# Three of six product halves on GpSimd in fp32, the other three on VectorE with one operand in PSUM

## The chip, the cores and the metric

One core of a Trainium2 chip runs the whole network. The metric is the device time of one execution in microseconds (us), the median of three runs. The engines are TensorE (PE, with PEld for its weight loads), VectorE (DVE), ScalarE (ACT), GpSimd (POOL) and SyncE (SP, which here issues DMAs).

## The reference, cut to what matters

The network is a chain of layers on x of 16 x 128 x 128: a mixture of experts, an attention, a low-rank adapter, a **quantised feed-forward net**, four more layers. The change lies in the quantised net alone. Its reference:

```python
def act_qdq(x):
    qmax = 2.0 ** (ACT_BITS - 1) - 1.0
    scale = jnp.maximum(jnp.max(jnp.abs(x)) / qmax, 1e-12)
    return jnp.clip(jnp.round(x / scale), -qmax - 1.0, qmax) * scale
...
up = act_qdq(x @ lpbq_dequant(w_up).T)
gate = act_qdq(x @ lpbq_dequant(w_gate).T)
sig = fixed_qdq_u16(jax.nn.sigmoid(gate))
gate = act_qdq(gate * sig)
o = act_qdq(gate * up)
return o @ lpbq_dequant(w_down).T
```

Here up and gate are 384 x 2048 numbers each; the second gate is called gated below, and gated * up is called ot. `act_qdq` has 16 bits and one scale for the whole tensor. Every one needs the largest absolute value of its whole tensor before one number of it can be rounded, so the stage is a row of barriers: a maximum over all columns, then over the partitions (a transpose on TensorE), then a scale and its reciprocal, then rounding.

## The kernel before, in words

The order of each engine's work is written out by hand, one function per engine (`tensor`, `scalar`, `vector`, `gpsimd`, `sync`); engines meet through counting semaphores, and each engine runs its instructions strictly in the order written. The semaphores of one writer share a counter (`LANES`), so the counts there follow the counts of the instructions.

Data of the stage: `UP[0..2]` and `GT[0..2]` are 128 x 2048 fp32 tiles in SBUF, which hold up and gate * sigmoid; `G16` and `U16Q` are int16 tiles of the same shapes. `BK[0..7]` are the eight PSUM banks of 128 x 512 words. `RQ` holds the reciprocals of the scales, `rq(2)` for up and `rq(3)` for gated. `pieces` cuts the three tiles into four: the two halves of tile 0 (1024 columns each), tile 1 and tile 2 (2048 columns each).

The steps around the change, with their lines:

- ACT, L1008: three instructions of 2048 columns scale and round `UP` to int16 (`U16Q`), signal `up16`. They need only the scale of up (`quant` 6), which is there early.
- DVE, L1519: multiplies gate and sigmoid and takes the maximum (signal `gated_ff`, 5 pieces). Then L1459, the transpose on PE (L588, `quant_turn(3)`), L1463 to L1475 make the scale of gated (`quant` 9), and L1542 signals `ffs` 3.
- DVE, L1544: rounds the first piece of `GT` to int16 itself. ACT, L1012: rounds the other three pieces (1024, 2048 and 2048 columns), signal `gated16`.
- DVE, L1548 and L1456 (`absmax`, a helper; called in L1550): for each of the four pieces the product of two int16 operands into fp32 `GT`, and then its maximum, signals `ot_ff` and `o_max`.
- PE, L610 to L615: waits for `o_max` 3, issues eight matmuls whose result nobody reads (L612), then the transpose of the maximum (L588, `quant_turn(4)`, which waits for `part_max` 5), and then six more such matmuls (L615).
- DVE, L1459, L1463 to L1475, L1556: the scale of ot. ACT, L1016: 12 x rounding to int16 of 512 columns. DVE, L1561 and L1563: the two fp16 parts of each. PE, L625: the down projection, 36 matmuls into `BK[0..3]`. DVE, L1567: adds to x.
- GpSimd, L1865 and L1867: halves the eight pieces of the last layer's weights into two fp16 parts. Pieces 0 to 3 are done at `l_lo` 4, pieces 4 to 7 wait for `o_lo` 12 (the last L1563).
- SP, L1942: loads expert weights for a later layer; those of experts 8 to 11 go into the tile `RC`, where `U16Q` lies, and wait for `ot_ff` 4. Behind them in SP's queue are `halve(6)` and `halve(7)`, which wait for GpSimd's pieces 4 and 5.

Of the kernel before, what the change touches and what calls it, by code (L numbers as in the profile page):

```python
# [10 lines left out]
I32 = mybir.dt.int32  # L11
I16 = mybir.dt.int16
U16 = mybir.dt.uint16
ALU = mybir.AluOpType
ACT = mybir.ActivationFunctionType
X_AX = mybir.AxisListType.X

NB, S, D = 16, 128, 128
# [9 lines left out]
MAGIC = 12582912.0  # L28
# [26 lines left out]
    (("x4mm", 4), ("spread", 4), ("xtmm", 4)),  # L55
    (("quant_mm", 5), ("pttmm", 4)),

    (("gelu", 48), ("u0", 4), ("v", 8), ("lora", 4), ("ff", 24), ("up16", 3), ("o16", 12), ("x3", 4), ("su", 16), ("z_hi", 64)),
    (("ret_a", 1), ("fw_hi", 3), ("wbot", 8), ("l16", 4), ("sig_gates", 1), ("sigmoid", 4), ("sig_top", 2), ("gated16", 3), ("z", 4), ("x5", 4), ("qv_out", 8)),
    (("aw_hi", 1), ("xn_hi", 4), ("sig16", 5), ("vv", 4), ("sqr", 4), ("exp", 16)),  # L60
    (("route_exp", 2), ("theta", 1), ("q_sh", 4), ("sq", 4), ("rt_exp", 3), ("ptt", 4)),
    (("x_hi", 4), ("wt16", 1), ("wts0", 1), ("wts", 3), ("ot_hi", 3)),

    (("gated", 48), ("weff", 4), ("sin", 32), ("fw_lo", 3), ("k", 4), ("g", 8), ("x1", 4), ("l_max", 4), ("l_lo", 4),
     ("ff_max", 24), ("gate16", 4), ("gated_ff", 5), ("ot_ff", 4), ("o_lo", 12), ("x2", 4), ("pp", 4), ("w2", 2), ("weighed", 64), ("zw", 16)),
    (("xg", 4), ("kadd", 4), ("l_hi", 4), ("gated16_0", 1), ("o_max", 4), ("o_hi", 12), ("x4", 4), ("zlo", 64)),
    (("q", 4), ("sn", 1), ("part_max", 5), ("x3_lo", 4), ("rs", 4)),
    (("cent", 4), ("whole_max", 5), ("z_lo", 4), ("nm", 8)),
    (("const", 2), ("sh_lo", 2), ("sim_sq", 1), ("ffs", 4), ("k_out", 4)),
# [43 lines left out]
def program(nc, A, out):  # L113
    with ExitStack() as ctx:
        def sb(name, shape, dt=F32):
            return ctx.enter_context(nc.sbuf_tensor(name, shape, dt))
# [16 lines left out]
        BK = [ctx.enter_context(nc.psum_tensor(f"bk{i}", [128, 512], F32)) for i in range(8)]  # L133
# [52 lines left out]
        def cc(c):  # L186
            return slice(512 * c, 512 * c + 512)
# [79 lines left out]
        Q_AT, Q_STEPS = (0, 1, 2, 3, 0), (2, 4, 6, 9, 12)  # L267
# [20 lines left out]
        MX = QS  # L288
# [92 lines left out]
        def tensor(e):  # L381
            q = Eng(e, by_home)
# [145 lines left out]
            for t2 in range(8):  # L528
# [5 lines left out]
                for h in range(2):  # L534
# [3 lines left out]
                    t = e.matmul(o, ON3[:, :], BV3[:, 3, :], start=False, stop=True)  # L538
# [3 lines left out]
            for c in range(4):  # L542
                q.wait_ge("sin", 32)
                q.wait_ge(*(("v", 5 + c) if c < 2 else ("kadd", c - 1)))
                for i in range(4):
                    t = e.matmul(BK[c % 2][:, bb_(i)], qkv[:, 4 * c + i, :], qqv[:, 4 * c + i, :], start=True, stop=True)
# [32 lines left out]
            for c in range(4):  # L579
                q.wait_ge("x1", c + 1)  # L580
                q.wait_ge(*(("wbot", 7 + c) if c < 2 else ("k", 4)))
                for i in range(4):
                    t = e.matmul(BK[c][:, bb_(i)], WEFF[:, bb_(4 * c + i)], XT[:, bb_(4 * c + i)], start=True, stop=True)
# [23 lines left out]
                t.then_inc(S("ffmm"), 1)  # L607
            for i in range(1, 4):
                quant_turn(i)
            q.wait_ge("o_max", 3)  # L610
            for _ in range(8):
                e.matmul(BK[6][:, :], FW16[:, 0, 0, :], FW16[:, 0, 0:4, :], start=True, stop=True)  # L612
            quant_turn(4)
# [233 lines left out]
        def scalar(e):  # L847
# [145 lines left out]
            for i, (j, h) in enumerate(pieces):  # L993
# [9 lines left out]
                if i == 3:  # L1003
                    q.wait_ge("sig_top", 1)
                    e.activation(S16TOP, STOP, ACT.Copy, scale=65536.0).then_inc(S("sig_top"), 1)
            for j in range(3):
                q.wait_ge("quant", Q_STEPS[2])
                e.activation(U16Q[j], UP[j], ACT.Identity, scale=rq(2)).then_inc(S("up16"), 1)  # L1008
            for i, (j, h) in enumerate(pieces):
                if i:  # L1010
                    q.wait_ge("quant", Q_STEPS[3])
                    e.activation(G16[j][:, h], GT[j][:, h], ACT.Identity, scale=rq(3)).then_inc(S("gated16"), 1)  # L1012
            for j in range(3):
                for c in range(4):
# [114 lines left out]
        def vector(e):  # L1129
# [325 lines left out]
            def absmax(dst, src):  # L1455
                return red(dst, src, X_AX, ALU.max, apply_absolute_value=True)  # L1456

            def quant_part(i, parts):
                red(QS[:, 56 + Q_AT[i]:57 + Q_AT[i]], parts, X_AX, ALU.max).then_inc(S("part_max"), 1)  # L1459
# [80 lines left out]
            quant_whole(3)  # L1540
            quant_scale(3, U2)
            ts(U3, QS[:, 62:63], QS[:, 63:64], 1.0 / QMAX, ALU.mult, ALU.mult).then_inc(S("ffs"), 1)  # L1542
            j, h = pieces[0]
            ts(G16[j][:, h], GT[j][:, h], rq(3), None, ALU.mult).then_inc(S("gated16_0"), 1)  # L1544
            for i, (j, h) in enumerate(pieces):
                q.wait_ge(*(("gated16", i) if i else ("gated16_0", 1)))
                q.wait_ge("up16", j + 1)
                tt(GT[j][:, h], G16[j][:, h], U16Q[j][:, h], ALU.mult).then_inc(S("ot_ff"), 1)  # L1548
                q.wait_ge("ot_ff", i + 1)
                absmax(MX[:, 30 + i:31 + i], GT[j][:, h]).then_inc(S("o_max"), 1)  # L1550
            q.wait_ge("o_max", 4)
            q.wait_ge("ffs", 3)
            quant_part(4, MX[:, 30:34])
            quant_whole(4)
            quant_scale(4, U3)
            ts(SLW, QS[:, 60:61], 1.0 / WS, None, ALU.mult).then_inc(S("ffs"), 1)  # L1556
# [259 lines left out]

        def gpsimd(e):
            q = Eng(e, by_home)
            q.wait_ge("expert_lo", 16)
            q.wait_ge("c2b", 16)  # L1820
            for k in range(5):
                e.tensor_tensor(sl8(6 + k), sl8(1), C2B[:, k, :].unsqueeze(1).to_broadcast([128, 16, 8]), ALU.mult).then_inc(S("chosen"), 1)
            q.wait_ge("l1w", 16)
            q.wait_ge("l1m", 16)
            e.tensor_tensor(L1W, L1W, L1M, ALU.mult).then_inc(S("l1p"), 1)

            q.wait_ge("pk1", 16)
            q.wait_ge("col", 16)
            cosT, sinT = pk1("cos"), pk1("sin")
            for i, n in enumerate(("qq", "qk")):  # L1830
                o = 4 * i
                e.tensor_scalar(ROPE[:, o, :], cosT, col(n + "w"), None, ALU.mult).then_inc(S("rope"), 1)
                e.tensor_scalar(ROPE[:, o + 1, :], sinT, col(n + "ws"), None, ALU.mult).then_inc(S("rope"), 1)
                e.tensor_scalar(ROPE[:, o + 2, :], cosT, col(n + "b"), None, ALU.mult).then_inc(S("rope"), 1)
                e.tensor_scalar(ROPE[:, o + 3, :], sinT, col(n + "bs"), None, ALU.mult).then_inc(S("rope"), 1)
                q.wait_ge("rope", 5 * i + 4)
                e.tensor_tensor(ROPE[:, o + 2, :], ROPE[:, o + 2, :], ROPE[:, o + 3, :], ALU.add).then_inc(S("rope"), 1)
            q.wait_ge("pk0", 16)
            e.tensor_tensor(ATT[:, 0, :], pk0("relb"), pk1("amask"), ALU.add).then_inc(S("relm"), 1)

            q.wait_ge("rope", 10)
            q.wait_ge("down", UNITS)
            q.wait_ge("q", 4)
            for c in range(4):
                q.wait_ge("base", c + 1)
                for l in range(4 * c, 4 * c + 4):
                    for o, dst in ((0, QQ), (4, QK)):
                        e.tensor_scalar(dst[:, bb_(l)], BASE[:, bb_(l)], ROPE[:, o, l:l + 1], ROPE[:, o + 2, l:l + 1], ALU.mult, ALU.add).then_inc(S("cos"), 1)  # L1848

            for i, b in enumerate(HALVED):  # L1850
                q.wait_ge("k", 4)
                q.wait_ge("c2_hi", i + 1)
                e.tensor_tensor(GU16[b][:, 1, :], GU[b], GU16[b][:, 0, :], ALU.subtract).then_inc(S("c2_lo"), 1)


            q.wait_ge("sin", 32)
            q.wait_ge("fw_lo", 3)
            q.wait_ge("wbot", 8)
            q.wait_ge("route", BIASES)
            for i in range(8):  # L1860
                src = XF[:, 1024 * (i % 2):1024 * (i % 2) + 1024]
                q.wait_ge(*(("l_lo", 4) if i < 4 else ("o_lo", 12)))
                hi, lo = P16[:, 0, 1024 * i:1024 * i + 1024], P16[:, 1, 1024 * i:1024 * i + 1024]
                q.wait_ge(f"w2_{i % 2}", 16 * (i // 2 + 1))
                e.tensor_scalar(hi, src, 1.0, 1.0, ALU.mult, ALU.mult).then_inc(S("p16_hi"), 1)  # L1865
                q.wait_ge("p16_hi", i + 1)
                e.tensor_tensor(lo, src, hi, ALU.subtract).then_inc(S("p16"), 1)  # L1867

        def sync(e):
# [69 lines left out]
            for i in range(6):  # L1939
                halve(i)  # L1940
            for b in (0, 1, 2, 3, 8, 9, 10, 11):
                q.wait_ge(*(("ffs", 3) if b < 4 else ("ot_ff", 4)))  # L1942
                chosen(b)
            halve(6)
            halve(7)
# [129 lines left out]
```

## Time and profile before

| | |
|---|---|
| time, median of 3 runs (lowest to highest) | 490.58 us (490.44 to 490.92) |
| the profiled execution: its time | 490.49 us |
| its span, first to last instruction | 488.7 us |
| mean granted TensorE clock | 0.965 |
| busy: PE | 438.8 us, 90% |
| busy: DVE | 410.8 us, 84% |
| busy: ACT | 244.6 us, 50% |
| busy: POOL | 62.7 us, 13% |

The span is the time between the first and the last instruction of the profiled execution; 1.8 us of its time lie outside. Busy shares are means over the whole span and tell little of a stage that is 14 us long: there, the order of the instructions and their waits count. All times below are in us from the start of the span unless marked ns.

### The profile page before, as it was taken

What the parts mean: (1) busy time and instruction counts of PE and PEld (TensorE: products, weight loads), DVE (VectorE), ACT (ScalarE), POOL (GpSimd) and SP (SyncE); (2) the same over time, 40 slices, a digit from 0 to 9 for tenths busy, and PEclk for the clock granted to TensorE, in tenths of its full rate; (3) what the DMA queues carried; (4) which work ended last, traced back from release to release, by engine and by line L of the source; (5) the groups of instructions that cost most, each with busy time, mean ns of one, the idle gap of its engine ahead of it and who ended that gap; (6) DMA issues with size and microseconds to landing.
All of it is one profiled execution on the core that took longest, in us unless ns stands there. A gap on an engine that the chain in (4) does not pass through costs nothing.

```text
span 488.7 us, 9719 instructions
## 1 busy us (share of the span) xinstructions
PE 438.8 (90%) x3791; PEld 304.3 (62%) x3791; DVE 410.8 (84%) x919; ACT 244.6 (50%) x446; POOL 62.7 (13%) x77
## 2 busy tenths in 40 slices
PE   8999999998899989401899899999999999999997
PEld 6447999987358754100279876667656666655676
DVE  6997889777797659999876689986998999989786
ACT  5976555473856629895655554336224222423110
POOL 0007000000590705500081000000000000000000
PEclk9999999999999999855999998999999999999999
DMA  8979997950560003403330016545863000000000
GB/s 271 352 303 392 386 382 301 372 240 23 150 173 1 1 0 129 130 0 129 130 98 1 1 43 221 170 178 180 280 237 97 7 12 7 5 7 7 6 7 28
DMA packets 24629, 66.71 MB, mean 137 GB/s; under 512 B 3108, under 2 KB 6567, under 8 KB 24455
## 3 DMA queue, kind: packets, MB, share of 16 engines
q1 hardware_dynamic: 24144, 65.98, 37.7%
q8 instruction: 30, 0.49, 0.4%
q10 hardware_dynamic: 438, 0.11, 0.1%
q14 instruction: 17, 0.13, 0.1%
HBM read 38.68 MB, written 1.18 MB: 82 GB/s over the span
## 4 chain that ended last, share of the span: by engine, by line
PE 25%; DVE 25%; issue 4%; ACT 1%; DVEq 0%
PE bk L758 8%; DVE XT L1741 6%; DVE X L1729 4%; PE bk L766 4%; DVE RA L1769 4%; PE bk L803 3%; PE bk L625 2%; DVE RA L1548 1%; DVE WK L1590 1%; PE bk L778 1%; PE bk L634 1%; PE bk L668 1%; PE bk L685 1%; DVE QS L1456 1%; PE bk L694 1%
## 5 line engine op out<-in xcount | busy, mean ns | idle before, releaser
L758 PE MATMUL bk<-X,RB 128*128 128x512 f16 x384 | 94.6, 383 | 0.6 <-DVE X L1729 0.4
L1061 ACT ACTIVATE X<-RA 128x512 f16<-128x512 f32 x64 | 40.3, 630 | 100.9 <-DVE RA L1769 84.7
L1741 DVE SCALAR_TENSOR_TENSOR XT<-bk,WK,XT 128x128 f32<-128x128 f32 x192 | 67.0, 349 | 5.4 <-issue 0.2
L758 PEld LDWEIGHTS bk<-X,RB 128*128 128x128 f16 x384 | 37.0, 98 | 42.3 <-DVE X L1729 1.6
L766 PEld LDWEIGHTS bk<-RB,X 128*128 128x128 f16 x768 | 48.4, 98 | 15.4 <-issue 0.6
L766 PE MATMUL bk<-RB,X 128*128 128x128 f16 x768 | 53.5, 220 | 0.0
L1729 DVE TENSOR_TENSOR X<-RA,X 128x512 f16<-128x512 f32 x64 | 43.9, 685 | 1.1 <-ACT X L1061 1.1
L899 ACT ACTIVATE WK<-bk 128x512 f32<-128x512 f32 x48 | 28.6, 595 | 27.5 <-PE bk L414 21.9
L803 PE MATMUL bk<-RB,RA 128*128 128x512 f16 x144 | 38.8, 379 | 0.9 <-DVE RA L1786 0.9
L1357 DVE SCALAR_TENSOR_TENSOR RB<-WK,WCOL,bk 128x512 f32<-128x512 f32 x32 | 23.7, 744 | 10.0 <-ACT WK L899 10.0
L414 PE MATMUL bk<-X,RC 128*128 128x128 f16 x480 | 29.7, 219 | 0.0
L1363 DVE TENSOR_TENSOR RB<-RB 128x512 f16<-128x512 f32 x36 | 25.7, 715 | 3.9 <-ACT RB L909 3.6
L414 PEld LDWEIGHTS bk<-X,RC 128*128 128x128 f16 x480 | 27.9, 98 | 0.9
L909 ACT ACTIVATE RB<-RB 128x512 f16<-128x512 f32 x36 | 22.4, 623 | 5.2 <-DVE RB L1357 5.0
L409 PE MATMUL bk<-X,STG 128*128 128x512 f16 x96 | 22.9, 379 | 0.5 <-DVE X L1171 0.4
L1456 DVE TENSOR_REDUCE QS<-RA 128x1 f32<-128x512 f32 (+2 forms) x28 | 22.4, 836 | 0.1
L588 PE MATMUL bk<-PK1T,QS 128*128 128x128 f32 x5 | 1.9, 384 | 20.5 <-DVE QS L1459 20.5
L1848 POOL TENSOR_SCALAR RA<-RA,ROPE 128x128 f32<-128x128 f32 x16 | 9.4, 586 | 81.4 <-ACT RA L929 81.4
L409 PEld LDWEIGHTS bk<-X,STG 128*128 128x128 f16 x96 | 9.2, 97 | 16.1 <-issue 5.2
L443 PE MATMUL bk<-RB,RC 128*128 128x128 f16 x240 | 16.6, 219 | 2.0 <-DVE RB L1363 2.0
L803 PEld LDWEIGHTS bk<-RB,RA 128*128 128x128 f16 x144 | 12.6, 98 | 7.3 <-DVE RA L1786 1.3
L1867 POOL TENSOR_TENSOR RB<-X,RB 128x1024 f16<-128x1024 f32 x8 | 17.1, 2132 | 0.7
(345 smaller groups left out, 887.3 us busy)
## 6 DMA issues: line engine op xcount, KB each, us to landing
RC<-RA SPq DMA_DIRECT2D x20, 768.0 KB, 5.2
STG<-RA SPq DMA_DIRECT2D x8, 768.0 KB, 5.3
RC<-expert_weights SPq DMA_DIRECT2D x22, 256.0 KB, 6.2
RC<-in_wx SPq DMA_DIRECT2D x7, 768.0 KB, 8.2
X<-in_w SPq DMA_DIRECT2D x8, 512.0 KB, 3.5
RA<-RA SPq DMA_DIRECT2D x4, 768.0 KB, 5.0
STG<-expert_weights SPq DMA_DIRECT2D x12, 256.0 KB, 6.5
QT<-expert_weights SPq DMA_DIRECT2D x8, 256.0 KB, 4.6
```

Source lines behind the costliest of these rows:

```text
L409: t = e.matmul(bank[:, :], W16[:, o:o + 128], X16[:, xp, cc(a)], start=(n == 0), stop=(n == 2))
L414: t = e.matmul(bank[:, bb_(jj)], w[:, o:o + 128], X16[:, xp, bb_(a)], start=(n == 0), stop=(n == 2))
L758: t = e.matmul(BK[m][:, :], P16[:, wp, wo:wo + 128], ZH[:, n % 4, xp, :], start=(e1 == 0 and i == 0), stop=(e1 == 15 and i == 2))
L766: t = e.matmul(BK[2][:, bb_(b)], ZH[:, n % 4, xp, bb_(b)], P16[:, wp, wo:wo + 128], start=(e1 == 0 and b == 0 and i == 0), stop=(e1 == 15 ...
L803: t = e.matmul(bank_o(n)[:, :], OT16[:, xp, bb_(4 * c + b)], P16[:, wp, 6144 + 512 * g:6656 + 512 * g], start=(i == 0), stop=(i == 2))
L899: e.activation(ge[u % 3], pair(k)[0][:, :], ACT.Gelu_apprx_tanh, scale=1.0 / WS).then_inc(S("gelu"), 1)
L1061: e.activation(ZH[:, r, 0, :], zf[r], ACT.Copy).then_inc(S("z_hi"), 1)
L1357: stt(hf[u % 3], ge[u % 3], w, pair(k)[1][:, :], ALU.mult, ALU.mult).then_inc(S("gated"), 1)
L1363: tt(H16[:, u % 3, 1, :], hf[u % 3], H16[:, u % 3, 0, :], ALU.subtract).then_inc(S("h_lo"), 1)
L1456: return red(dst, src, X_AX, ALU.max, apply_absolute_value=True)
L1729: tt(ZH[:, n % 4, 1, :], zf[n % 4], ZH[:, n % 4, 0, :], ALU.subtract).then_inc(S("zlo"), 1)
L1741: stt(XT[:, bb_(t_)], bank_o(n)[:, bb_(i)], RW[:, t_, e1:e1 + 1], XT[:, bb_(t_)], ALU.mult, ALU.add).then_inc(S("acc"), 1)
```

## The change

The stage's six halves of 1024 columns are numbered 0 to 5 (tile `i // 2`, first or second half). Halves 1, 3 and 5 (`BY_POOL`) go to GpSimd, halves 0, 2 and 4 (`BY_VECTOR`) stay on VectorE.

- ACT rounds up for a VectorE half into int32 words in two PSUM banks (two instructions of 512 columns), and for a GpSimd half into fp32 in place by adding the constant `MAGIC` = 12582912 (one instruction, scale and bias both read from memory). GpSimd subtracts `MAGIC` again.
- ACT rounds gated for halves 1, 3 and 5 by adding `MAGIC`, for halves 2 and 4 to int16 as before. For halves 1 and 5 ACT also subtracts `MAGIC` (a second instruction, behind a wait for the first), for half 3 GpSimd does. That is seven instructions instead of three.
- VectorE makes each of its products in two instructions of 512 columns, and the maximum of all six halves, in the order product 0, max 0, product 2, max 2, max 1, product 4, max 4, max 3, max 5.
- PE's eight matmuls ahead of `quant_turn(4)` wait for `o_max` 5 instead of 3. SP's load of experts 8 to 11 waits for `o_max` 6 instead of `ot_ff` 4. GpSimd sets the two constants with memsets at the start of the program.

```diff
@@ tensor
-            q.wait_ge("o_max", 3)
+            q.wait_ge("o_max", 5)
             for _ in range(8):
                 e.matmul(BK[6][:, :], FW16[:, 0, 0, :], FW16[:, 0, 0:4, :], start=True, stop=True)
             quant_turn(4)
@@ scalar
-            for j in range(3):
+            q.wait_ge("magic", 2)
+            for i in range(6):
+                j, h = halves[i]
                 q.wait_ge("quant", Q_STEPS[2])
-                e.activation(U16Q[j], UP[j], ACT.Identity, scale=rq(2)).then_inc(S("up16"), 1)
-            for i, (j, h) in enumerate(pieces):
-                if i:
-                    q.wait_ge("quant", Q_STEPS[3])
+                if i in BY_POOL:
+                    t = e.activation(UP[j][:, h], UP[j][:, h], ACT.Identity, bias=MAGC, scale=rq(2))
+                else:
+                    for n in range(2):
+                        t = e.activation(U16P[i][n], UP[j][:, cc(n)], ACT.Identity, scale=rq(2))
+                t.then_inc(S("up16"), 1)
+            for n, (i, off) in enumerate(((1, 0), (1, 1), (2, 0), (3, 0), (4, 0), (5, 0), (5, 1))):
+                j, h = halves[i]
+                q.wait_ge("quant", Q_STEPS[3])
+                if off:
+                    q.wait_ge("gated16", n)
+                    e.activation(GT[j][:, h], GT[j][:, h], ACT.Identity, bias=MAGN).then_inc(S("gated16"), 1)
+                elif i in BY_POOL:
+                    e.activation(GT[j][:, h], GT[j][:, h], ACT.Identity, bias=MAGC, scale=rq(3)).then_inc(S("gated16"), 1)
+                else:
                     e.activation(G16[j][:, h], GT[j][:, h], ACT.Identity, scale=rq(3)).then_inc(S("gated16"), 1)
@@ vector
-            for i, (j, h) in enumerate(pieces):
-                q.wait_ge(*(("gated16", i) if i else ("gated16_0", 1)))
-                q.wait_ge("up16", j + 1)
-                tt(GT[j][:, h], G16[j][:, h], U16Q[j][:, h], ALU.mult).then_inc(S("ot_ff"), 1)
-                q.wait_ge("ot_ff", i + 1)
-                absmax(MX[:, 30 + i:31 + i], GT[j][:, h]).then_inc(S("o_max"), 1)
+            GATED = {0: ("gated16_0", 1), 2: ("gated16", 3), 4: ("gated16", 5)}
+            def ot_product(i):
+                j = halves[i][0]
+                q.wait_ge(*GATED[i])
+                q.wait_ge("up16", i + 1)
+                for n in range(2):
+                    t = tt(GT[j][:, cc(n)], G16[j][:, cc(n)], U16P[i][n], ALU.mult)
+                t.then_inc(S("ot_ff"), 1)
+            def ot_max(i):
+                j, h = halves[i]
+                q.wait_ge("ot_pool" if i in BY_POOL else "ot_ff", i // 2 + 1)
+                absmax(MX[:, 30 + i:31 + i], GT[j][:, h]).then_inc(S("o_max"), 1)
...
@@ gpsimd, ahead of piece 4 of L1865
+                    for m, n in enumerate(BY_POOL):
+                        j, h = halves[n]
+                        q.wait_ge("up16", n + 1)
+                        q.wait_ge("gated_ff", 5)
+                        e.tensor_scalar(UP[j][:, h], UP[j][:, h], MAGIC, None, ALU.subtract).then_inc(S("pool_whole"), 1)
+                    for m, n in enumerate(BY_POOL):
+                        j, h = halves[n]
+                        q.wait_ge("gated16", (2, 4, 7)[m])
+                        if n == 3:
+                            e.tensor_scalar(GT[j][:, h], GT[j][:, h], MAGIC, None, ALU.subtract).then_inc(S("pool_whole"), 1)
+                        q.wait_ge("pool_whole", (1, 4, 4)[m])
+                        e.tensor_tensor(GT[j][:, h], UP[j][:, h], GT[j][:, h], ALU.mult).then_inc(S("ot_pool"), 1)
@@ sync
-                q.wait_ge(*(("ffs", 3) if b < 4 else ("ot_ff", 4)))
+                q.wait_ge(*(("ffs", 3) if b < 4 else ("o_max", 6)))
```

## Rows read from the trace of the kernel before

**Rows 1.** Chain that ended last, 220 to 238: start us, us, what.
```profile
220.88 1.24 DVE RA L1548
...
232.50 2.30 DVE QS L1456
...
235.03 0.34 PE bk L588
```
**Rows 2.** Timeline of DVE: start us, us, engine, line, operation, out<-in.
```profile
220.10 0.74 DVE L1544 TENSOR_SCALAR WK<-RA,RQ 128x1024 int16<-128x1024 f32 x1
...
222.14 1.22 DVE L1456 TENSOR_REDUCE QS<-RA 128x1 f32<-128x1024 f32 x1
223.28 1.22 DVE L1548 TENSOR_TENSOR RA<-WK,RC 128x1024 f32<-128x1024 int16 x1
...
227.98 2.29 DVE L1456 TENSOR_REDUCE QS<-RA 128x1 f32<-128x2048 f32 x1
```
**Rows 3.** Timeline of ACT from 215 to 245.
```profile
215.84 5.77 ACT L1008 ACTIVATE RC<-RA,RQ 128x2048 int16<-128x2048 f32 x3
221.52 4.92 ACT L1012 ACTIVATE WK<-RA,RQ 128x1024 int16<-128x1024 f32 x3
236.41 7.46 ACT L1016 ACTIVATE WK<-RA,RQ 128x512 int16<-128x512 f32 x12 [9.98 <-DVE RQ L1475]
```
**Rows 4.** Timeline of PE from 215 to 240.
```profile
218.43 0.48 PE L588 MATMUL bk<-PK1T,QS 128*128 128x128 f32 x1 [11.20 <-DVE QS L1459]
230.32 3.60 PE L612 MATMUL bk<-FW 128*128 128x512 f16 x8 [11.41 <-DVE QS L1456]
235.03 0.32 PE L588 MATMUL bk<-PK1T,QS 128*128 128x128 f32 x1 [1.11 <-DVE QS L1459]
235.19 1.46 PE L615 MATMUL bk<-FW 128*128 128x512 f16 x6
237.98 8.12 PE L625 MATMUL bk<-RA,FW 128*128 128x512 f16 x36 [1.33 <-DVE RA L1563]
```
**Rows 5.** Stretches of 0.4 us: length, PE busy (matmuls), granted clock, DMA.
```profile
234.20:234.60 0.40, 0.00 (x0) 0.77 0.71 284
234.60:235.00 0.40, 0.00 (x0) 1.00 1.02 415
```
**Rows 6.** Group of DVE by form: busy us, mean ns, idle before.
```profile
L1769 DVE TENSOR_TENSOR RA<-RA,bk 128x512 f32<-128x512 f32 x4 | 2.7, 679 | 0.0
```
**Rows 7.** Groups of ACT by form.
```profile
L1002 ACT ACTIVATE WK<-RA 128x1024 uint16<-128x1024 f32 x2 | 2.1, 1057 | 0.1
L1012 ACT ACTIVATE WK<-RA,RQ 128x1024 int16<-128x1024 f32 x1 | 1.1, 1132 | 0.0
...
L1028 ACT ACTIVATE RA<-bk 128x512 f32<-128x512 f32 x4 | 2.4, 597 | 2.8 <-PE bk L652 2.7
```
**Rows 8.** Groups of POOL by form.
```profile
L1865 POOL TENSOR_SCALAR RB<-X 128x1024 f16<-128x1024 f32 x8 | 8.4, 1044 | 61.4 <-DVE RA L1563 42.8 <-DMA X<-in_w 18.6
L1825 POOL TENSOR_TENSOR RB<-RB 128x1024 f32<-128x1024 f32 x1 | 2.4, 2354 | 0.0
```
**Rows 9.** Timeline of DVE and POOL, two places where both work in SBUF.
```profile
39.84 1.71 DVE L1363 TENSOR_TENSOR RB<-RB 128x512 f16<-128x512 f32 x1
...
135.08 0.45 POOL L1848 TENSOR_SCALAR RA<-RA,ROPE 128x128 f32<-128x128 f32 x1
135.50 1.54 POOL L1848 TENSOR_SCALAR X<-RA,ROPE 128x128 f32<-128x128 f32 x1
```
**Rows 10.** Timeline of SP, POOL and PE: what the later stages take from here.
```profile
232.63 1.88 SPq L1921 DMA_DIRECT2D RC<-in_w  x4
...
256.94 2.13 POOL L1867 TENSOR_TENSOR RB<-X,RB 128x1024 f16<-128x1024 f32 x1
...
273.21 1.14 PE L685 MATMUL bk<-XT,RC 128*128 128x128 f32 x8
...
293.01 2.74 PE L758 MATMUL bk<-X,RB 128*128 128x512 f16 x6 [0.38 <-DVE X L1729]
```

More of the change, by code:

```diff
@@ L56 @@
     (("quant_mm", 5), ("pttmm", 4)),
-    (("gelu", 48), ("u0", 4), ("v", 8), ("lora", 4), ("ff", 24), ("up16", 3), ("o16", 12), ("x3", 4), ("su", 16), ("z_hi", 64)),
-    (("ret_a", 1), ("fw_hi", 3), ("wbot", 8), ("l16", 4), ("sig_gates", 1), ("sigmoid", 4), ("sig_top", 2), ("gated16", 3), ("z", 4), ("x5", 4), ("qv_out", 8)),
+    (("gelu", 48), ("u0", 4), ("v", 8), ("lora", 4), ("ff", 24), ("up16", 6), ("o16", 12), ("x3", 4), ("su", 16), ("z_hi", 64)),
+    (("ret_a", 1), ("fw_hi", 3), ("wbot", 8), ("l16", 4), ("sig_gates", 1), ("sigmoid", 4), ("sig_top", 2), ("gated16", 7), ("z", 4), ("x5", 4), ("qv_out", 8)),
     (("aw_hi", 1), ("xn_hi", 4), ("sig16", 5), ("vv", 4), ("sqr", 4), ("exp", 16)),
@@ L64 @@
     (("gated", 48), ("weff", 4), ("sin", 32), ("fw_lo", 3), ("k", 4), ("g", 8), ("x1", 4), ("l_max", 4), ("l_lo", 4),
-     ("ff_max", 24), ("gate16", 4), ("gated_ff", 5), ("ot_ff", 4), ("o_lo", 12), ("x2", 4), ("pp", 4), ("w2", 2), ("weighed", 64), ("zw", 16)),
-    (("xg", 4), ("kadd", 4), ("l_hi", 4), ("gated16_0", 1), ("o_max", 4), ("o_hi", 12), ("x4", 4), ("zlo", 64)),
+     ("ff_max", 24), ("gate16", 4), ("gated_ff", 5), ("ot_ff", 3), ("o_lo", 12), ("x2", 4), ("pp", 4), ("w2", 2), ("weighed", 64), ("zw", 16)),
+    (("xg", 4), ("kadd", 4), ("l_hi", 4), ("gated16_0", 1), ("o_max", 6), ("o_hi", 12), ("x4", 4), ("zlo", 64)),
     (("q", 4), ("sn", 1), ("part_max", 5), ("x3_lo", 4), ("rs", 4)),
@@ L169, in program @@
         RQ = sb("RQ", [128, 10])
+        MG = sb("MG", [128, 2])
+        MAGC, MAGN = MG[:, 0:1], MG[:, 1:2]
         def pk0(n):
@@ L301, in program @@
         pieces = [(0, slice(0, 1024)), (0, slice(1024, 2048)), (1, slice(0, 2048)), (2, slice(0, 2048))]
+        halves = [(i // 2, slice(1024 * (i % 2), 1024 * (i % 2) + 1024)) for i in range(6)]
+        BY_POOL, BY_VECTOR = (1, 3, 5), (0, 2, 4)
+        U16P = {i: [BK[i + n][:, :].bitcast(I32) for n in range(2)] for i in BY_VECTOR}
         GALL = WK[:, :, :].rearrange("p a n -> p (a n)")[:, 0:3072].bitcast(I16)
@@ L1542, in vector @@
             ts(U3, QS[:, 62:63], QS[:, 63:64], 1.0 / QMAX, ALU.mult, ALU.mult).then_inc(S("ffs"), 1)
-            j, h = pieces[0]
-            ts(G16[j][:, h], GT[j][:, h], rq(3), None, ALU.mult).then_inc(S("gated16_0"), 1)
-            for i, (j, h) in enumerate(pieces):
-                q.wait_ge(*(("gated16", i) if i else ("gated16_0", 1)))
-                q.wait_ge("up16", j + 1)
-                tt(GT[j][:, h], G16[j][:, h], U16Q[j][:, h], ALU.mult).then_inc(S("ot_ff"), 1)
-                q.wait_ge("ot_ff", i + 1)
-                absmax(MX[:, 30 + i:31 + i], GT[j][:, h]).then_inc(S("o_max"), 1)
-            q.wait_ge("o_max", 4)
+            GATED = {0: ("gated16_0", 1), 2: ("gated16", 3), 4: ("gated16", 5)}
[10 more added lines that the diff above has]
+                absmax(MX[:, 30 + i:31 + i], GT[j][:, h]).then_inc(S("o_max"), 1)
+            j, h = halves[0]
+            ts(G16[j][:, h], GT[j][:, h], rq(3), None, ALU.mult).then_inc(S("gated16_0"), 1)
+            ot_product(0)
+            ot_max(0)
+            ot_product(2)
+            ot_max(2)
+            ot_max(1)
+            ot_product(4)
+            ot_max(4)
+            ot_max(3)
+            ot_max(5)
+            q.wait_ge("o_max", 6)
             q.wait_ge("ffs", 3)
-            quant_part(4, MX[:, 30:34])
+            quant_part(4, MX[:, 30:36])
             quant_whole(4)
@@ L1818, in gpsimd @@
             q = Eng(e, by_home)
+            e.memset(MAGC, MAGIC).then_inc(S("magic"), 1)
+            e.memset(MAGN, -MAGIC).then_inc(S("magic"), 1)
             q.wait_ge("expert_lo", 16)
@@ L1860, in gpsimd @@
             for i in range(8):
+                if i == 4:
+                    for m, n in enumerate(BY_POOL):
[10 more added lines that the diff above has]
+                        e.tensor_tensor(GT[j][:, h], UP[j][:, h], GT[j][:, h], ALU.mult).then_inc(S("ot_pool"), 1)
                 src = XF[:, 1024 * (i % 2):1024 * (i % 2) + 1024]
```

## The prediction

> **What bounds the kernel now.** I read the chain that ended last first. Between 220.9 and 234.8 it is on VectorE alone: four products and four maxima with no idle time between them [rows 1, 2]. The stage takes 234.8 (232.50 + 2.30) less 220.88 = 13.9 us; then come the maximum over the partitions, the transpose on PE at 235.03 and the scale. ScalarE is not on it: it rounds up from 215.84 to 221.5 and gated from 221.52 to 226.4, and then sits idle for 10 us [rows 3]. GpSimd is idle throughout. PE does one thing that matters below: at 230.32 it begins eight matmuls that nobody reads, 3.60 us of them, and is through at 233.92, so that it idles for 1.11 us before the transpose is ready [rows 4]. The start at 230.32 is the end of the third maximum, 227.98 + 2.29 [rows 2]. The granted clock is at its lower level (1.2 GHz) through all eight and reaches 2.4 GHz only between 234.2 and 234.6, some 4.1 us after the first of them [rows 5].
>
> The profiled execution took 490.49 us, 0.09 below the median of 490.58. I sum against 490.49.
>
> **The change, part by part.**
>
> *VectorE's work.* A product of 1024 columns takes 1.22 us, and its maximum, which waits for it, starts 1.26 after it; the next product starts 1.14 after the maximum, since two instructions with no wait between them overlap by some 0.08 (220.88, 222.14, 223.28) [rows 1, 2]. The new product has one operand in PSUM, as int32, in two instructions of 512. No row shows that; the nearest is a 128x512 fp32 product with one PSUM operand, 0.68 us [rows 6], so 0.60 + 0.68 + 0.04 for the wait behind it = 1.32 us. From below it is 1.22 (the operand in SBUF), from above about 1.45 (0.06 more for each instruction). Three products at 1.32 and six maxima at 1.14 are 10.8 us, where 13.9 were: **3.1 us of work leave VectorE**.
>
> *ScalarE before the products.* One instruction of 1024 columns takes 1.06 us with constant scale and 1.13 with a scale from memory, so a pointer costs about 0.08; one with both scale and bias from memory I take at 1.22, and its successor starts 0.09 before its end (215.84 + 5.77 = 221.61 against 221.52) [rows 3, 7]. 512 columns with a scale from memory come every 0.61 (7.46 / 12) [rows 3]. Up is then three times (2 x 0.61 + 1.13) = 7.1 us against 5.7: it ends at 222.9, **1.4 us later**. How fast ScalarE writes PSUM no row shows. The cheapest row of 512 columns is 0.60 (source in PSUM, no pointer) [rows 7], 0.50 from start to start, and would save 6 x 0.11 = 0.7 us. I keep 0.61, since the pointer and the SBUF source remain, and 0.7 as the bound.
>
> The Trainium skill ("ScalarE: Activation LUTs", section "What happens when an exp ACTIVATE runs") says that ScalarE writes PSUM faster than SBUF. No run here shows it; by it the sum would lean to that bound.
>
> *ScalarE's gated, and who waits.* In its queue: half 1 plus MAGIC 222.9 to 224.15; half 1 minus MAGIC, behind a wait on the first, 224.2 to 225.3; half 2 225.2 to 226.35; half 3 to 227.5; half 4 to 228.5; half 5 to 229.65; its subtraction 229.7 to 230.8. Two instructions for half 1 stand **ahead** of half 2, and VectorE's second product waits for half 2. VectorE has its own rounding done at 220.84 [rows 2], product 0 at 222.2 and maximum 0 at 223.4, and then idles until 226.4: a new wait of 3.0 us (226.4 - 223.4), which takes nearly all of the 3.1 that it saved. Behind it are queued all of its later products and maxima.
>
> *GpSimd.* Its product of 1024 fp32 columns takes 2.35 us, with fp16 output 2.13; one-operand work takes 1.04 [rows 8, 10]. Subtracting MAGIC from up: three times 1.04 between 218.3 and 223.9, hidden, since gated is not ready. Product 1: 225.4 to 227.8. Half 3: 227.8 to 228.8, product 3 to 231.25. Product 5: to 233.6 (its gated is ready at 230.8).
>
> *VectorE again, with these.* Product 2 226.4, maximum 2 227.7, maximum 1 228.85, product 4 230.0, maximum 4 231.3, maximum 3 232.45 to 233.7, maximum 5 at 233.65 (just as GpSimd is done) to 234.87. The last maximum ends about 0.1 us later than the 234.8 of now: **the move by itself is worth nothing**.
>
> *PE's eight matmuls.* This is where I see the loss. They now wait for the fifth maximum, 233.7 instead of 230.32, and the transpose stands behind them in PE's queue. The pieces are smaller now: between the signal and the end of the last maximum lie 1.2 us, where the piece of 2048 columns left 4.5. The eight need about 3.4 us at the lower clock (3.60 less a tail of some 0.2) [rows 4], so the transpose starts at 237.15 instead of 235.03: **+2.1 us**. The clock rose 4.1 us after the first of them [rows 5], so the transpose would still be at the lower level, 0.48 us where it takes 0.32 now [rows 4]: +0.16. The six matmuls after it fit, at either clock, into the 2.95 us that scale, rounding and splitting take from there (235.03 to 237.98) [rows 4].
>
> *What costs nothing.* The two memsets on GpSimd are at the start of the program, 200 us before use. GpSimd's last four weight pieces keep their wait for `o_lo` 12 and shift with the chain; they are done at 259.1 and first used at 293.0, 34 us of cover [rows 10]. SP's four loads move from 232.63 to about 235, and are used at 273.2 [rows 10]; the two issues behind them wait for GpSimd anyway.
>
> Sum: 490.49 + 2.12 + 0.16 = **492.8 us**. After the transpose each step waits for the one before it, so I pass the delay on to the end undiminished.
>
> **The rivals.**
>
> *GpSimd and VectorE block each other.* VectorE's 128x512 product took 1.71 us instead of some 0.69 at 39.84, while GpSimd's product ran, and a GpSimd instruction of 0.45 took 1.54 beside a VectorE product [rows 9]: about 1.1 us for a meeting. If each of GpSimd's three products loses 1.1, they end at 228.9, 233.5 and 236.9; maximum 3 ends at 234.7, the eight matmuls at 238.1, maximum 5 at 238.1 and the transpose starts at 238.4: +3.4 + 0.16, **494.0 us**. Against it: in both places VectorE read two operands in SBUF, and here it reads one there, or makes a maximum. The Trainium skill ("SBUF — State Buffer", section "Who interferes with whom") says that a VectorE instruction with at most one SBUF input outside the two-port modes does not contend; by that the loss is none.
>
> *Not slower: the clock rises among the eight.* At 2.4 GHz they take 0.24 each (1.46 / 6) [rows 4]. Were the clock up from the first, the transpose would start at 233.7 + 1.95 = 235.65, **491.1 us**; for under 1 us of loss the rise must come within 0.65 us of their start. Against it: now it took 4.1 us, and PE is idle for at least 11 us before, as now [rows 4]. A rise midway gives 491.9.
>
> *Faster: ScalarE does not hold VectorE up.* The place is VectorE's wait before product 2, the price up to 3.0 us, and it decides only if half 2 is rounded by 223.4. Then maximum 3 ends at 230.7 and the last one at 231.9, yet the eight matmuls still end at 234.1: 489.7 with the 0.16, within 0.2% of now. Only with the clock up as well would the transpose start at 232.7, at **488.1 us**. Seven instructions' durations speak against it, and GpSimd would be late too.
>
> **How the numbers follow.** The forecast, from 491.9 to 493.2 with the bounds above (-0.7 for the PSUM writes, +0.3 for the products, and a clock rise midway), gets 0.58; the blocking 0.18; the early clock or other losses of the delay on the way, landing within 0.2%, 0.14; faster 0.10. 0.2% is 1.0 us, about what a measurement of this kernel can tell from no change. Slower is the first two: 0.76. The range of 8 in 10 goes from 490.9 (part of the third case) to 494.4 (the blocking with its own spread).
>
> **What would show it.** In the changed profile: ACT's L1012 successors start at 222.9 (now 221.5); VectorE idles some 3 us behind its first maximum, released by ACT; GpSimd's products take 2.1 to 2.4 us; the last maximum ends near 234.9; PE's eight unread matmuls start at 233.7 and the transpose follows them directly, released by nothing but PE itself, near 237.1. I am wrong if the transpose starts within 0.4 us of the last maximum's end, if GpSimd's products take over 3 us, or if the distance from the transpose to the end of the span is not the 253.7 us of now (488.7 - 235.03).

## The result, and the profile after

The changed kernel takes 494.8 us (median of 5 runs, 494.64 to 496.19) where the kernel before takes 490.58 (490.38 to 490.92): ratio 1.0091, 95% interval 1.0076 to 1.0105. It is **4.2 us slower**. The forecast was slower by 2.3 us, 492.8, with a range to 494.4: the direction is right, the size is not, and the time lies just outside the range. Single executions near 495 us turn up in the kernel before (2 in 19 in the later runs) and in one of the kernels below (2 in 12); a median does not feel them, a ratio's interval does.

| | before | after |
|---|---|---|
| time, median | 490.58 us | 494.8 us |
| span of the profiled execution | 488.7 us | 492.9 us |
| mean granted TensorE clock | 0.965 | 0.958 |
| busy: DVE / ACT / POOL | 410.8 / 244.6 / 62.7 us | 409.9 / 249.1 / 81.2 us |

The page already has the surprise: GpSimd is busy for 18.5 us more. Three products of 2.35 and four subtractions of 1.04 would be 11.2.

The timeline of VectorE in the stage, which answers to [rows 2] (start us, us, engine, line, operation, out<-in, and in brackets the idle time before and what ended it):

```profile
219.75 1.59 DVE L1580 TENSOR_SCALAR WK<-RA,RQ 128x1024 int16<-128x1024 f32 x1
221.38 1.28 DVE L1571 TENSOR_TENSOR RA<-WK,bk 128x512 f32<-128x512 int16 x2
222.70 1.22 DVE L1477 TENSOR_REDUCE QS<-RA 128x1 f32<-128x1024 f32 x1
226.03 1.28 DVE L1571 TENSOR_TENSOR RA<-WK,bk 128x512 f32<-128x512 int16 x2 [2.11 <-ACT WK L1033]
...
229.06 1.22 DVE L1477 TENSOR_REDUCE QS<-RA 128x1 f32<-128x1024 f32 x1 [0.48 <-POOL RA L1914]
230.19 1.27 DVE L1571 TENSOR_TENSOR RA<-WK,bk 128x512 f32<-128x512 int16 x2
...
234.22 1.22 DVE L1477 TENSOR_REDUCE QS<-RA 128x1 f32<-128x1024 f32 x1 [1.50 <-POOL RA L1914]
236.53 1.22 DVE L1477 TENSOR_REDUCE QS<-RA 128x1 f32<-128x1024 f32 x1 [1.09 <-POOL RA L1914]
```

Four waits stand where the kernel before had none: one for ScalarE, as forecast, and three for GpSimd, which were not. The last maximum ends at 237.75, not at 234.87. The chain that ended last, which answers to [rows 1] (start us, us, what), now runs through GpSimd:

```profile
218.03 4.68 POOL RA L1907 x2
222.71 1.23 issue
223.94 2.77 POOL RA L1907
226.71 2.32 POOL RA L1914
229.03 2.74 POOL RA L1912
...
231.84 2.35 POOL RA L1914
234.20 0.02 issue
234.22 1.23 DVE QS L1477
235.45 0.05 issue
235.50 3.60 PE bk L620 x8
239.09 0.23 PE bk L596
```

Two links matter. L1907 and L1912, the subtractions of MAGIC, take 2.8 us each (one of the four 3.20). And behind maximum 3 (234.22) the chain does not go to the last maximum but to PE: the eight unread matmuls, then the transpose. The groups of GpSimd, against [rows 8]:

```profile
L1907 POOL TENSOR_SCALAR RA<-RA 128x1024 f32<-128x1024 f32 x3 | 8.7, 2915 | 15.4 <-ACT RA L1019 15.4
L1919 POOL TENSOR_SCALAR RB<-X 128x1024 f16<-128x1024 f32 x8 | 8.4, 1048 | 32.5 <-DMA X<-in_w 19.7 <-DVE RA L1602 12.8
L1914 POOL TENSOR_TENSOR RA<-RA 128x1024 f32<-128x1024 f32 x3 | 7.0, 2347 | 0.1
...
L1912 POOL TENSOR_SCALAR RA<-RA 128x1024 f32<-128x1024 f32 x1 | 2.8, 2764 | 0.0
```

The products take what was forecast (2.35). The subtractions are tensor_scalar instructions of 128x1024 like L1919, and take over 2.6 times as long. The timeline of PE, against [rows 4]:

```profile
235.50 3.60 PE L620 MATMUL bk<-FW 128*128 128x512 f16 x8 [16.94 <-DVE QS L1477]
238.89 0.42 PE L596 MATMUL bk<-PK1T,QS 128*128 128x128 f32 x1
239.10 1.73 PE L623 MATMUL bk<-FW 128*128 128x512 f16 x6
241.93 8.12 PE L633 MATMUL bk<-RA,FW 128*128 128x512 f16 x36 [1.10 <-DVE RA L1602]
```

The transpose has no bracket: it waited for nothing but PE, though the maximum it turns was ready at 237.94. It starts at 238.89 instead of 235.03, 3.86 us later, in a run whose stage began 0.35 us earlier (219.75 against 220.10). That is 4.2 us more from VectorE's first rounding to the transpose (19.14 against 14.93), the whole of the loss.

### The profile page after: what moved, and what is told of

The parts are those of the page before. It is cut to its first block, busy times and chain, and to the rows that moved or that the text cites. A ratio compares the mean times of both kernels' runs of the same rounds, so it can differ in the third digit from the quotient of the medians.

```text
span 492.9 us, 9745 instructions
## 1 busy us (share of the span) xinstructions
PE 438.2 (89%) x3791; PEld 304.9 (62%) x3791; DVE 409.9 (83%) x923; ACT 249.1 (51%) x456; POOL 81.2 (16%) x86
## 4 chain that ended last, share of the span: by engine, by line
PE 56%; DVE 29%; ACT 6%; issue 5%; POOL 3%; DMA 0%; DVEq 0%; ACTq 0%; POOLq 0%
PE bk L766 9%; PE bk L422 6%; DVE XT L1780 6%; PE bk L774 5%; PE bk L417 4%; DVE QS L1477 3%; DVE X L1768 3%; PE bk L451 3%; PE bk L811 3%; DVE RA L1808 2%; PE bk L435 2%; PE bk L633 2%; PE bk L545 2%; POOL RA L1907 2%; DVE RB L1384 1%
## 5 line engine op out<-in xcount | busy, mean ns | idle before, releaser
L1384 DVE TENSOR_TENSOR RB<-RB 128x512 f16<-128x512 f32 x36 | 26.8, 744 | 3.9 <-ACT RB L917 3.6
L1477 DVE TENSOR_REDUCE QS<-RA 128x1 f32<-128x512 f32 (+1 forms) x30 | 22.7, 791 | 3.2 <-POOL RA L1914 3.1
L620 PE MATMUL bk<-FW 128*128 128x512 f16 x8 | 3.6, 631 | 16.9 <-DVE QS L1477 16.9
```

The lines of the kernel that those rows point to most:

```text
L1384: tt(H16[:, u % 3, 1, :], hf[u % 3], H16[:, u % 3, 0, :], ALU.subtract).then_inc(S("h_lo"), 1)
```

## The experiments

**The forms of one GpSimd instruction.** What makes L1907 slow where L1919 is fast? It has one operation instead of two, it subtracts, it writes fp32, and VectorE works beside it. The probe put ten forms, three times each, on 128x1024 in an idle part of SBUF, ahead of GpSimd's share (A_ and B_ are fp32, H_ is fp16). In the diff the wait ahead of each and the signal at its end are left out, and at the end the subtraction in place and a product; the loads of expert weights wait for the probe too. In the diffs behind it the signals are left out likewise.

```diff
+                e.tensor_scalar(B_, A_, MAGIC, None, ALU.subtract)
+                e.tensor_scalar(B_, A_, MAGIC, 1.0, ALU.subtract, ALU.mult)
+                e.tensor_scalar(B_, A_, 1.0, None, ALU.mult)
+                e.tensor_scalar(B_, A_, 1.0, 1.0, ALU.mult, ALU.mult)
+                e.tensor_scalar(B_, A_, 1.0, 1.0, ALU.mult, ALU.add)
+                e.tensor_scalar(B_, A_, 1.0, None, ALU.add)
+                e.tensor_scalar(H_, A_, 1.0, None, ALU.mult)
+                e.tensor_scalar(H_, A_, 1.0, 1.0, ALU.mult, ALU.mult)
...
```

> Thirty extra GpSimd instructions of 1024 columns, ahead of its share of the products, so its time is no measure (some 50 us longer). Theory A (the form with one operation is slow, whatever it computes): every tensor_scalar with one operation takes 2.8 to 2.9 us, every one with two operations 1.0 to 1.1, with fp32 and with fp16 output. Rival B (subtraction is slow): the two subtractions take 2.8 in either form, multiplications 1.05. Rival C (fp32 output is slow): all with fp32 output take 2.8, those with fp16 output 1.05. Rival D (it was blocking by VectorE): all take about 1.05 where VectorE stands still.

The third round, in the timeline of GpSimd, the lines in the order of the diff. VectorE stood still in it: it waited for 54.75 us, until 288.88.

```profile
254.60 2.77 POOL L1909 TENSOR_SCALAR RC<-RC 128x1024 f32<-128x1024 f32 x1
257.45 3.64 POOL L1911 TENSOR_SCALAR RC<-RC 128x1024 f32<-128x1024 f32 x1
261.17 2.78 POOL L1913 TENSOR_SCALAR RC<-RC 128x1024 f32<-128x1024 f32 x1
264.03 1.05 POOL L1915 TENSOR_SCALAR RC<-RC 128x1024 f32<-128x1024 f32 x1
265.16 1.05 POOL L1917 TENSOR_SCALAR RC<-RC 128x1024 f32<-128x1024 f32 x1
266.29 2.77 POOL L1919 TENSOR_SCALAR RC<-RC 128x1024 f32<-128x1024 f32 x1
269.14 2.77 POOL L1921 TENSOR_SCALAR RC<-RC 128x1024 f16<-128x1024 f32 x1
272.00 1.05 POOL L1923 TENSOR_SCALAR RC<-RC 128x1024 f16<-128x1024 f32 x1
```

The two forms not shown took 2.77 (subtraction in place) and 2.34 (product). Output type (rival C) and VectorE (rival D) do not matter: 2.77 stands with fp16 output too, and with VectorE idle. Subtraction (rival B) is not the whole cause, since a lone multiplication takes 2.78. Theory A holds for the one-operation forms, 2.77 whatever they compute, but it fails at one point: subtract-then-multiply, with two operations, is the slowest of all at 3.64. Fast are only multiply-multiply and multiply-add. Why these forms are slow and those fast no run shows. (What was expected of the next kernels was written before this was known; two of them still go by theory A.)

VectorE is not the cause, but the first round, beside VectorE at work, shows that it can add to it: the subtraction took 3.98 us there and subtract-multiply 4.48, while VectorE's four roundings took 6.62 us, where they take 3.80 in the kernel before.

**Subtract, then times 1.0.**

```diff
-    e.tensor_scalar(UP[j][:, h], UP[j][:, h], MAGIC, None, ALU.subtract)
+    e.tensor_scalar(UP[j][:, h], UP[j][:, h], MAGIC, 1.0, ALU.subtract, ALU.mult)
... (the same for GT)
```

> The changed kernel with GpSimd's four subtractions of MAGIC written with a second operation (times 1.0). Theory A: they fall from 2.8 to 1.05 us each, GpSimd's first product starts at 225.05 instead of 226.67, the last maximum ends near 234.5 instead of 237.75, PE's eight unread matmuls start at 233.4 and hold the transpose until 236.8 instead of 238.9: 492.7 us. Rivals B to D: no change, 494.8.

It took 497.81 us, ratio 1.0142 (1.0128 to 1.0157): slower by another 3 us where 2.1 less was expected. The timeline of GpSimd shows the probe's 3.64 in place:

```profile
218.48 10.83 POOL L1907 TENSOR_SCALAR RA<-RA 128x1024 f32<-128x1024 f32 x3 [15.49 <-ACT RA L1019]
...
231.59 3.64 POOL L1912 TENSOR_SCALAR RA<-RA 128x1024 f32<-128x1024 f32 x1
```

So the run raised the suspected cost alone: the three subtractions from up take 10.83 us where they took 8.68, that of half 3 takes 3.64 where it took 2.76, 3.0 us more together and 3.0 us more in the end.

**PE's wait one maximum earlier, GpSimd left slow.**

```diff
-            q.wait_ge("o_max", 5)
+            q.wait_ge("o_max", 4)
```

> The changed kernel with PE's eight unread matmuls waiting for o_max 4 instead of 5, GpSimd as slow as it was. Theory (the transpose stands behind them in PE's queue): they start near 232.8 and end before the last maximum, the transpose starts at 238.0 instead of 238.9, 493.9 us. Rival (the transpose is late for another reason): 494.8. If the clock falls or rises late because of the gap of 1.6 us between them and the transpose, the down projection is slower and takes back up to 2 us.

494.11 us (6 runs, 493.26 to 494.82), ratio 1.0070 (1.0056 to 1.0083), close to the 493.9 expected. By the times alone it is hardly told from the 494.8 of the changed kernel, whose interval overlaps; the profile shows the change. On PE:

```profile
232.86 3.59 PE L620 MATMUL bk<-FW 128*128 128x512 f16 x8 [14.23 <-DVE QS L1477]
238.08 0.48 PE L596 MATMUL bk<-PK1T,QS 128*128 128x128 f32 x1 [1.62 <-DVE QS L1480]
238.35 2.77 PE L623 MATMUL bk<-FW 128*128 128x512 f16 x6
```

The transpose now waits for VectorE and starts 0.8 us earlier (0.9 from VectorE's rounding on). So in the changed kernel, where GpSimd is late, the eight matmuls cost 0.8 to 0.9 us and not 2.1: the late last maximum covers the rest. The clock stayed at its lower level until 240.8 here (0.48 for the transpose, 2.77 for the six); the down projection took its 8.12 us all the same.

**Both, with the wrong form.** Subtract-then-multiply and PE's wait at `o_max` 3.

> Two-operation form, and PE's wait back at o_max 3. Theory: both losses gone, the transpose starts 0.2 us after a last maximum that ends near 234.5, where the kernel before had it at 235.0 and its stage began 0.35 us later: 490.6 us, within 0.2% of the kernel before, since what VectorE saves goes into its wait for ScalarE (2.1 us seen). Rival (the move of the products is worth its 3 us once these two are mended): 487.6 to 488.5.

497.2 us, ratio 1.0138 (1.0123 to 1.0152). The premise, GpSimd at 1.05, did not hold, so this tells nothing of the theory; the same step with the right form stands below.

**Times 1.0, plus -MAGIC.** The same numbers come out.

```diff
-    e.tensor_scalar(UP[j][:, h], UP[j][:, h], MAGIC, None, ALU.subtract)
+    e.tensor_scalar(UP[j][:, h], UP[j][:, h], 1.0, -MAGIC, ALU.mult, ALU.add)
...
-    e.tensor_scalar(GT[j][:, h], GT[j][:, h], MAGIC, None, ALU.subtract)
+    e.tensor_scalar(GT[j][:, h], GT[j][:, h], 1.0, -MAGIC, ALU.mult, ALU.add)
```

> The changed kernel with GpSimd's four subtractions written as times 1.0 plus -MAGIC, the form that took 1.05 us. Theory (the forecast's sum was right but for the 2.8 us of this one row): GpSimd's first product starts within 0.2 us of ScalarE's half 1, the last maximum ends near 234.5, PE's eight unread matmuls start near 233.4 and the transpose follows at 236.8: 492.7 us (+2.1 on the kernel before). Rival (GpSimd's products or VectorE are held up by something else too): it stays above 493.7.

492.5 us (6 runs), ratio 1.0036 (1.0024 to 1.0048). On VectorE, GpSimd and PE:

```profile
226.27 1.28 DVE L1571 TENSOR_TENSOR RA<-WK,bk 128x512 f32<-128x512 int16 x2 [2.96 <-ACT WK L1033]
...
231.16 3.48 DVE L1477 TENSOR_REDUCE QS<-RA 128x1 f32<-128x1024 f32 x3
...
225.28 2.35 POOL L1914 TENSOR_TENSOR RA<-RA 128x1024 f32<-128x1024 f32 x1 [1.27 <-ACT RA L1029]
227.60 1.04 POOL L1912 TENSOR_SCALAR RA<-RA 128x1024 f32<-128x1024 f32 x1
...
233.56 3.59 PE L620 MATMUL bk<-FW 128*128 128x512 f16 x8 [14.77 <-DVE QS L1477]
236.95 0.42 PE L596 MATMUL bk<-PK1T,QS 128*128 128x128 f32 x1
```

This is the forecast's stage, row by row: VectorE waits 2.96 us for ScalarE and never for GpSimd; the last three maxima run in one piece to 234.64 (forecast 234.87); the eight matmuls start at 233.56 (233.7); the transpose follows at 236.95 (237.15), 2.1 us after its data (234.67 + 0.16). The form of four instructions was 2.3 us of the loss (494.8 less 492.5; 2.1, if each is taken against the kernel before in its own runs, 490.58 and 490.42).

**And PE's wait back at `o_max` 3.**

```diff
-            q.wait_ge("o_max", 5)
+            q.wait_ge("o_max", 3)
```

> The same with PE's wait back at o_max 3. Theory: the transpose starts 0.2 us after the last maximum, near 234.7, 490.6 us, within 0.2% of the kernel before: VectorE saves 3 us of work and waits 3 us for ScalarE. The difference to the kernel with o_max 5 is 2.1 us, the price of the eight matmuls ahead of the transpose. Rival (the order of the queues costs nothing when GpSimd is fast): both kernels give the same time.

490.17 us (12 runs), ratio 1.0009 (0.998 to 1.0038); the kernel before has 490.42 in these runs, and the kernel with `o_max` 5 lies 2.3 us higher. In its timeline of PE the transpose is released by VectorE again:

```profile
229.53 3.60 PE L620 MATMUL bk<-FW 128*128 128x512 f16 x8 [11.20 <-DVE QS L1477]
234.45 0.47 PE L596 MATMUL bk<-PK1T,QS 128*128 128x128 f32 x1 [1.32 <-DVE QS L1480]
234.72 2.77 PE L623 MATMUL bk<-FW 128*128 128x512 f16 x6
```

The rest of the loss is gone, and the move itself is worth nothing that can be measured: by the times within 0.4%, by the profile within 0.01 us, since from VectorE's rounding to the transpose it is 14.92 us (234.45 - 219.53) where it was 14.93.

**Is it ScalarE that eats VectorE's saving?** Half 5 goes back to VectorE, and ScalarE's order is changed so that half 2 is rounded first (left out in the middle: half 1 minus MAGIC). Two things more go with it, not shown in the diff: VectorE takes maximum 4 ahead of maximum 1 and maximum 3 last, and ScalarE has six instructions on gated instead of seven. PE waits at `o_max` 3, and GpSimd has the fast form:

```diff
-        BY_POOL, BY_VECTOR = (1, 3, 5), (0, 2, 4)
+        BY_POOL, BY_VECTOR = (1, 3), (0, 2, 4, 5)
...
+            for i in range(4):
+                up_whole(i)
+            gated_whole(2)
+            gated_whole(1)
...
+            up_whole(4)
+            gated_whole(4)
+            gated_whole(3)
+            up_whole(5)
+            gated_whole(5)
```

> As the last one, but half 5 back on VectorE (its up in PSUM banks 0 and 1, once product 0 has read them) and ScalarE's order changed: up of halves 0 to 3, then gated of half 2, half 1 with its subtraction, up and gated of half 4, gated of half 3, up and gated of half 5. Theory (VectorE's wait for ScalarE ate the saving): VectorE waits under 1 us in the stage, the last maximum ends near 233.2 to 233.6, 489.3 us, 1.2 below the kernel before. Rival (the stage is bound by the sum of ScalarE's work, whatever its order): no faster than the kernel before, 490.4 or more.

489.4 us (8 runs), ratio 0.9974 (0.9963 to 0.9985): **faster than both kernels**, 1.0 us below the kernel before (490.42 in these runs). The waits of VectorE's products are nearly gone:

```profile
221.06 1.28 DVE L1587 TENSOR_TENSOR RA<-WK,bk 128x512 f32<-128x512 int16 x2
...
223.51 1.27 DVE L1587 TENSOR_TENSOR RA<-WK,bk 128x512 f32<-128x512 int16 x2
...
226.47 1.29 DVE L1587 TENSOR_TENSOR RA<-WK,bk 128x512 f32<-128x512 int16 x2 [0.43 <-ACT WK L1036]
...
230.06 1.27 DVE L1587 TENSOR_TENSOR RA<-WK,bk 128x512 f32<-128x512 int16 x2
```

0.43 us of waiting for ScalarE where 2.96 were. The transpose starts at 233.96, 1.07 us earlier than in the kernel before [rows 4]. How much comes from ScalarE's order, from its shorter work, from half 5 or from VectorE's order was not tried.

**Without the eight matmuls.** The kernel with `o_max` 3, but L612's eight left out.

```diff
-            q.wait_ge("o_max", 3)
-            for _ in range(8):
-                e.matmul(BK[6][:, :], FW16[:, 0, 0, :], FW16[:, 0, 0:4, :], start=True, stop=True)
```

> The kernel with the two-operation form and PE's wait at o_max 3, but with the eight unread matmuls ahead of the transpose left out (the six behind it stay). Theory (they are there for the clock): the transpose starts when it did, but the clock rises only about 4 us after it, some 1 us into the down projection, which takes 8.6 to 9.0 us instead of 8.1: 0.5 to 1.0 us slower. Rival (they bring nothing, and only cost where they stand in the way): the same time as with them.

491.08 us (12 runs; the kernel before has 490.72 in these), ratio 0.9996 (0.9974 to 1.0018) to the kernel before, against 1.0009 (0.998 to 1.0038) with them: not told apart by the times. The profile shows the slower down projection, and more of it than the 8.6 to 9.0 us expected:

```profile
234.78 2.77 PE L620 MATMUL bk<-FW 128*128 128x512 f16 x6
237.61 9.37 PE L630 MATMUL bk<-RA,FW 128*128 128x512 f16 x36
```

The transpose and the six matmuls are the same with and without the eight (0.48 and 2.77 against 0.47 and 2.77, at the lower level). The difference comes behind them. The stretch in which the clock rises (length, PE busy, granted clock, DMA) is this with the eight:

```profile
237.00:237.80 0.80, 0.74 (x4) 0.73 0.96 369
```

and this without them:

```profile
240.20:241.00 0.80, 0.80 (x5) 0.80 0.02 8
```

So it rises some 3 us later, well inside the down projection, which takes 9.37 us instead of 8.12. The eight bring up to 1.25 us where they are in time. Of this, 0.9 us arrives at the end in the two profiled executions (from the transpose to the end of the span 254.8 us against 253.9); by the times of all executions it isn't shown.

**The runs side by side.** From the start of VectorE's rounding of half 0 to the start of the transpose, by the profile, and the median against that of the kernel before in the same runs:

| kernel | rounding to transpose | more than before | median, more than before |
|---|---|---|---|
| before | 14.93 us | | |
| changed | 19.14 us | 4.21 | 4.2 |
| changed, `o_max` 4 | 18.26 us | 3.33 | 3.4 |
| subtract and times 1.0 | 22.14 us | 7.21 | 7.1 |
| the same, `o_max` 3 | 21.24 us | 6.31 | 6.5 |
| times 1.0 plus -MAGIC | 16.96 us | 2.03 | 2.1 |
| the same, `o_max` 3 | 14.92 us | -0.01 | -0.2 |
| the same, without the eight | 14.90 us | -0.03 | 0.4 |
| half 5 on VectorE, ScalarE's new order | 13.68 us | -1.25 | -1.0 |

## Why the prediction was right or wrong

- **The step that failed** is the one on GpSimd: "one-operand work takes 1.04", and with it "Subtracting MAGIC from up: three times 1.04 ... hidden" and "Half 3: 227.8 to 228.8". It measured 2.77, and 3.20 once. The row it came from (L1865, [rows 8]) has the same size and engine but another form, multiply-multiply with two constants and fp16 output, and the new instructions have one operation and subtract. No row of GpSimd in the kernel before has one operation at that size. The prediction gave the PSUM writes, the products and the clock a bound each, and this number none; nor do its signs of being wrong name it, and none of the three came (the distance to the end, 254.0 us against 253.7, is dealt with below).
- What it changed in the sum: the forecast has the transpose 2.12 us later, and with VectorE's rounding as the start it came 4.21 later. Three subtractions of 2.8 are no longer hidden behind ScalarE (GpSimd's first product starts at 226.67 instead of some 225.1), and that of half 3 stands between two products. With the fast form the kernel takes 492.5, where the forecast was 492.8.
- **The eight matmuls ahead of the transpose: right**, in place, start and size. 2.1 us were forecast for a GpSimd in time; the pair of kernels with `o_max` 5 and 3 gives 2.3 by the times and 2.04 by the profiles. With the slow form only 0.8 to 0.9 of them show, because the last maximum is late as well. So the two losses overlap: the form alone costs 3.3 to 3.4 us (`o_max` 4), the eight alone 2.0 to 2.3, and both together 4.2.
- **"The move by itself is worth nothing": right**, 1.0009 (0.998 to 1.0038). The 3.0 us wait before product 2 measured 2.96 with the fast form. In the changed kernel it is 2.11, since VectorE's own rounding (L1580) took 1.59 us instead of 0.74 and filled the rest.
- ScalarE: 1.23 us with scale and bias from memory (forecast 1.22); two writes of 512 columns into PSUM 1.28 together, 0.61 from start to start, as from SBUF to SBUF. The bound of 0.7 us below was not needed. The Trainium skill ("ScalarE: Activation LUTs", section "Step-by-step: what each stage is for", which stands behind the one that the prediction names) says that ScalarE writes PSUM faster than SBUF. Here that shows only as 0.67 against 0.71 us for one instruction; the start-to-start time is the same.
- VectorE's product with one operand in PSUM: 1.28 for two, forecast 1.28.
- **Rival "GpSimd and VectorE block each other"** (0.18) named nearly the right time, 494.0, and the right place, GpSimd's products starting late, for the wrong reason. GpSimd's products took 2.35 us in every kernel, beside VectorE's work. That agrees with the rule of the Trainium skill ("SBUF — State Buffer", section "Who interferes with whom") that a VectorE instruction with at most one SBUF input, outside the two-port modes, does not contend. Blocking did occur at another place, where VectorE rounds half 0 (L1580, 1.59 us instead of 0.74): one of GpSimd's subtractions beside it took 3.20 instead of 2.77, and these 0.43 us lie on the chain.
- **The clock: right here, in part by luck.** It rose some 4 us after the first of the eight (235.50), as it had before [rows 5]; the transpose took 0.42 and not 0.48, and the down projection its 8.12 as before. So the +0.16 of the forecast measured 0.10. But 4 us is no constant of this kernel: counted from the first of the eight, the clock rose after 3.7 to 4.9 us in five of the kernels (before, changed, both with `o_max` 5, and the last one), after 7.9 us in two (`o_max` 4 with the slow form, `o_max` 3 with the fast one), and after 12.5 us in one (the slowest form, `o_max` 3). What decides it no run shows. In stretches of 0.6 us (length, PE busy, granted clock, DMA):

```profile
238.80:239.40 0.60, 0.60 (x3) 0.50 0.99 133
239.40:240.00 0.60, 0.60 (x3) 0.80 0.83 287
```

- From the transpose to the end of the span it is 254.0 us (492.9 - 238.9) where it was 253.7, so the delay is passed on undiminished. The moved loads (issued from 237.91, used at 277.17) and GpSimd's last weight pieces (done at 263.7, used at 296.9) cost nothing that shows.
- One limit is off in the rival on the clock: by its own numbers the rise must come within some 0.85 us, not 0.65. Nothing hung on it.

## What to carry to other kernels

A duration belongs to a form (operations, operand kinds, one or two of them), not to an engine and a size: when the nearest row has another form, give it a bound like any unknown, and a sign by which you would see it. Work placed ahead of a critical instruction in the same queue, such as matmuls that only keep the clock up, must be timed against the *last* signal it hides behind; cutting the last piece of work from 4.5 to 1.2 us takes its cover away. And work that leaves the bound engine gains only what the next supplier can follow: here VectorE gained nothing while it waited for ScalarE's queue, and 1 us once that queue was reordered and shortened and half 5 was back on VectorE.

## What was not expected of the hardware

GpSimd's tensor_scalar on 128x1024 fp32: multiply-multiply and multiply-add 1.05 us; a single operation (subtract, multiply or add) 2.77 to 2.78; subtract-multiply 3.64. fp16 output changes nothing, nor does writing in place.

VectorE's rounding of 128x1024 (L1580) took 0.74 us in most of the kernels, and 1.59 to 1.60 in the changed one and in that with `o_max` 4. In the changed one it starts at 219.75, during GpSimd's first subtraction (218.03 to 220.80), and ends 0.54 us after it; the second subtraction, from 220.77, is the one of 3.20 us. That the two held each other up is likely, and the first round of the probe agrees, where VectorE's roundings took 6.62 us instead of 3.80. It does not explain the rest: with the 3.64 us form running beside it all the time (218.48 to 222.12), L1580 took 0.74, and so it did in the probe beside a single subtraction (225.48 to 228.25), which took its 2.77. What tells these cases apart was not pursued. The VectorE side cost nothing, since it waited for ScalarE right after; the GpSimd side cost 0.43 us of the chain.
